# Four reordered places, and the last tiles less their mean on ScalarE beside GpSimd's power

## What is computed

```python
x = x + layernorm(attn0(layernorm(x)))   # attention over the 8 heads of a group, token by token
x = x + layernorm(ffn0(layernorm(x)))    # ternary weights, sigmoid gate
x = x + layernorm(attn1(layernorm(x)))   # 16 heads of 32, causal, rotary embedding
x = x + layernorm(ffn1(layernorm(x)))    # silu gate, 2 of each 4 hidden values kept

def layernorm(x):
    return (x - mean(x)) / sqrt(var(x) + 1e-5)

def ffn1(x):                             # I = 2048
    h = silu(x @ w_gate) * (x @ w_up)
    return keep_two_largest_of_four(h) @ w_down
```

## Time and profile before

| | us |
|---|---|
| median of 3 runs | 1380.36 |
| lowest, highest | 1379.38, 1383.88 |
| the profiled execution | 1379.57 |
| its span in the profile | 1377.8 |
| TensorE busy | 1321.3 (96%) |
| VectorE busy | 981.6 (71%) |
| GpSimd busy | 697.2 (51%) |
| ScalarE busy | 659.4 (48%) |

### The profile page before, as it was taken

How to read it: one execution, slowest core, us unless ns; L and a number is a source line. 1 busy time by engine, 2 the same in 40 slices (tenths; PEclk the granted TensorE clock), 3 DMA queues, 4 the chain that set the end, 5 groups by cost and what they waited for, 6 DMA issues and landing times.

```text
span 1377.8 us, 19437 instructions
## 1 busy us (share of the span) xinstructions
PE 1321.3 (96%) x7181; PEld 911.1 (66%) x7206; DVE 981.6 (71%) x1961; ACT 659.4 (48%) x1149; POOL 697.2 (51%) x836
## 2 busy tenths in 40 slices
PE   6989999999999899999999999999999999999998
PEld 5876446556455455555555457888888788878886
DVE  5898675665767867777666543896779677867787
ACT  6665332232324554455554565645454545455442
POOL 2576231412312424233334276785788668857874
PEclk9999999999999999999999999999999999999999
DMA  9100210103213213034012323122324232322310
GB/s 333 80 1 1 77 62 16 62 31 110 66 46 101 62 41 78 21 108 120 24 55 55 124 93 147 68 94 90 133 83 152 98 134 94 143 104 100 118 36 31
DMA packets 46270, 116.86 MB, mean 85 GB/s; under 512 B 3420, under 2 KB 4448, under 8 KB 42336
## 3 DMA queue, kind: packets, MB, share of 16 engines
q1 hardware_dynamic: 45104, 114.31, 24.5%
q10 hardware_dynamic: 1072, 1.31, 0.3%
HBM read 92.28 MB, written 23.07 MB: 84 GB/s over the span
## 4 chain that ended last, share of the span: by engine, by line
PE 78%; DVE 14%; ACT 4%; issue 2%; POOL 1%; DMA 0%; SPq 0%; POOLq 0%; DVEq 0%; ACTq 0%
PE PS L1796 76%; DVE PS L919 2%; DVE SM L702 2%; PE PS L1805 1%; DVE cm L686 1%; DVE hm L695 1%; DVE SM L698 1%; ACT EX L1369 1%; DVE qb L692 1%; DVE SM L703 1%; DVE tm L686 0%; DVE qa L692 0%; DVE xT L695 0%; DVE SM L692 0%; DVE hm L686 0%
## 5 line engine op out<-in xcount | busy, mean ns | idle before, releaser
L1369 ACT ACTIVATE EX<-PS 128x512 f32<-128x512 f32 (+3 forms) x384 | 169.8, 492 | 134.2 <-PE PS L1796 132.6
L1600 POOL TENSOR_TENSOR ws_g<-rw,ws_g 128x512 fp32r<-128x512 f32 x64 | 134.5, 2102 | 117.5 <-ACT ws_g L1186 117.5
L1600 POOL TENSOR_TENSOR SM<-SM 128x1 f32<-128x1 f32 x128 | 85.4, 667 | 200.5 <-DVE SM L692 197.8
L919 DVE CUSTOM_DVE_ANT_0 PS<-PS,MW 128x128 f32<-128x128 f32 (+3 forms) x256 | 122.3, 503 | 61.6 <-PE PS L1796 61.2
L1796 PE MATMUL PS<-KG,QG 96*128 96x512 f32 (+3 forms) x384 | 134.3, 380 | 17.3 <-DVE SM L919 7.4
L1715 POOL TENSOR_SCALAR_AFFINE_SELECT EX<-EX 128x128 f32<-128x128 f32 x256 | 74.7, 302 | 146.2 <-ACT EX L1369 143.8
L1507 ACT ACTIVATE ab<-hm 128x512 f32<-128x512 f32 x64 | 40.5, 633 | 208.8 <-DVE hm L686 208.8
L1796 PE MATMUL PS<-QG,KG 98*128 98x512 f32 (+3 forms) x384 | 130.3, 374 | 2.1 <-ACT EX L1369 1.7
L686 DVE TENSOR_TENSOR cm<-cm 128x512 bf16<-128x512 bf16 (+1 forms) x136 | 128.3, 973 | 2.4
L1796 PE MATMUL PS<-ws_d,HH 128*128 128x512 f32 x528 | 125.4, 389 | 0.0
L1796 PEld LDWEIGHTS PS<-QG,KG 98*128 98x128 f32 x384 | 69.1, 189 | 69.5 <-issue 43.8
(11 more groups left out here) (204 smaller groups left out, 2782.0 us busy)
## 6 DMA issues: line engine op xcount, KB each, us to landing
rw<-in_L_ffn_w_gate SPq DMA_DIRECT2D x16, 1024.0 KB, 5.0
rw<-in_L_ffn_w_up SPq DMA_DIRECT2D x16, 1024.0 KB, 6.4
rw<-in_L_ffn_w_down SPq DMA_DIRECT2D x16, 1024.0 KB, 7.2
QG<-qs SPq DMA_DIRECT2D x48, 256.0 KB, 4.3
raw<-in_L_ffn_w SPq DMA_DIRECT2D x3, 2816.0 KB, 11.7
qs<-stg SPq DMA_DIRECT2D x16, 512.0 KB, 3.5
xA<-xs SPq DMA_DIRECT2D x2, 2048.0 KB, 7.5
ys<-xA SPq DMA_DIRECT2D x4, 1024.0 KB, 4.2
```

What stands on the lines that cost most here:

```text
L919: last = e.tensor_tensor_reduce(out=p, in0=p, in1=MW[:, 512 - k1 + k0:512], scale=1.0, scalar=BIG, op0=ALU.add, op1=ALU.max, accum_out=m1)
L1369: e.activation(EX[:, n % 16, 0:W], PS[:, score_bank(n), 0:W], ACT.Exp, scale=ISQ, bias=0.0).then_inc(S["ex"], 1)
L1600: return e.tensor_tensor(out, a, b, op)
```

## The change

Five edits:

1. VectorE, last feed-forward: phase 2 of `sparse` is cut in two. The casts stay phase 2 and now stand ahead of the two `turn4`; the subtractions become phase 3 and stay behind them. This differs only at s = 14, 30 and 46.
2. GpSimd, last projection: `stats` of tile step - 2 ahead of `residual` of tile step - 3.
3. ScalarE, second attention: `drain(14)` at n = 358 instead of 360. VectorE's drain 14 stays at 360.
4. ScalarE, second attention: the event `("t3", i)` at its four n stands ahead of `exp(n)` instead of behind it.
5. The last four tiles: VectorE also writes -mean (semaphore `mneg`); GpSimd takes only the power; ScalarE writes the tile less its mean, waiting for `mneg` and not for GpSimd; VectorE then multiplies by the power and adds `xb` in one operation, waiting for both.

```diff
@@ dve_program
+            rounded = [0] * 4
...
-                        n = did(e.tensor_copy(sparse4(q, 0), h[:, r, :]))
+                        rounded[r] = did(e.tensor_copy(sparse4(q, 0), h[:, r, :]))
+                if phase == 3:
                     for r in range(4):
                         q = 4 * g + r
-                        w.wait_ge(S["dvs"], n - 3 + r)
+                        w.wait_ge(S["dvs"], rounded[r])
                         tt(sparse4(q, 1), h[:, r, :], sparse4(q, 0), ALU.subtract).then_inc(S["hh4"], 1)
...
+                if g >= 1 and s % 4 == 2:
+                    sparse(g - 1, 2)
 
                 if k < 3 and s % 16 in (14, 15):
                     i = 4 * (k + 1) + 2 * (s % 16 - 14)
                     turn4(i)
                     turn4(i + 1)
                 if g >= 1 and s % 4 == 2:
-                    sparse(g - 1, 2)
+                    sparse(g - 1, 3)
...
                 stats(124 + i, PS[:, i, :], EPS, "mv8")
+                ts1(col(124 + i, 5), col(124 + i, 0), -1.0, ALU.mult).then_inc(S["mneg"], 1)
...
                 w.wait_ge(S["sn5"], 13 + i)
-                tt(xb[1][:, i, :], xb[1][:, i, :], row4("p", 12 + i), ALU.add).then_inc(S["xo"], 1)
+                w.wait_ge(S["rs8"], 13 + i)
+                stt(xb[1][:, i, :], row4("p", 12 + i), col(124 + i, 4), xb[1][:, i, :], ALU.mult, ALU.add).then_inc(
+                    S["xo"], 1)
@@ act_program
+                    if n in turn_at:
+                        event(("t3", 12 + turn_at.index(n)))
                     exp(n)
                     for t in behind[n]:
-                        event(t)
+                        if t[0] != "t3":
+                            event(t)
...
-                    if n in drain_at:
+                    if n in drain_at and drain_at[n] < 14:
                         drain(drain_at[n])
+                    if n == done_at[14] + 6:
+                        drain(14)
...
-                w.wait_ge(S["rs8"], 13 + i)
+                w.wait_ge(S["mneg"], i + 1)
                 wait_row4("p", 12 + i)
-                norm(row4("p", 12 + i), PS[:, i, :], 124 + i).then_inc(S["sn5"], 1)
+                e.activation(row4("p", 12 + i), PS[:, i, :], ACT.Identity, scale=1.0, bias=col(124 + i, 5)).then_inc(
+                    S["sn5"], 1)
@@ pool_program
-                for k, i in stages(8, 4, step):
-                    if k == 3:
-                        residual(1, i)
-                    if k == 2:
-                        stats(88 + i, "mv6", "rs6", 8 + i)
+                if 2 <= step < 10:
+                    stats(86 + step, "mv6", "rs6", 6 + step)
+                if 3 <= step < 11:
+                    residual(1, step - 3)
...
-                stats(124 + i, "mv8", "rs8", 12 + i)
+                w.wait_ge(S["mv8"], 13 + i)
+                tt(col(124 + i, 4), col(124 + i, 2), mhalf[:, 0:1], ALU.pow).then_inc(S["rs8"], 1)
```

More of the change, by code:

```diff
@@ L45 @@
 pj ue rb rp qh ql d_w0 d_w1 d_k0 d_k1 d_k2 d_k3 d_q00 d_q01 d_q10 d_q11 vj vt vtp va
-sx mxr nm mtp mtl d_m0 d_m1 st ex sel pvd oe de rd oo d_xc cwh cwl
+sx mxr nm mtp mtl d_m0 d_m1 st ex sel pvd oe de rd oo mneg d_xc cwh cwl
 ehi ot ep pc mv6 rs6 en ey d_ys0 d_ys1
```

## The result

| | before | after |
|---|---|---|
| median of 4 runs, us | 1380.12 | 1374.02 |
| lowest, highest, us | 1379.38, 1383.88 | 1373.81, 1374.28 |
| the profiled execution, us | 1379.57 | 1374.02 |
| its span, us | 1377.8 | 1372.3 |

The ratio of after to before is 0.995, with a 95% interval of 0.9937 to 0.9964. The change makes the kernel faster by 0.36 to 0.63%. In part that is luck: terms were wrong in both directions, as the marks on the way show, and one mark that the prediction itself named as a sign of being wrong was missed (edit 3). The table gives when the same instruction starts in the two traces, and what the change gained in the stretch that ends there.

A forecast was written before the change was run, and what follows sets the result against it. TensorE was taken to bound the kernel, so only its waits and the chain behind its last matmul could pay. Terms -2.8 - 1.1 - 0.25 + 0.05 - 1.05 = -5.15 us gave 1374.4, with the median allowance 1374.8; range 1373.3 to 1377.0.

The forecast's parts named there:

- -2.8: Last feed-forward, s = 14, 30, 46: earlier casts end TensorE's three stalls for `hm`, -2.8 us, bounds 2.2 and 2.8.
- (a): At s = 14, 30, 46 another wait takes over, above all ScalarE's queue: 1376.2 (half lost) or 1377.6 us; chance 0.13.
- (e): Last feed-forward: without pauses TensorE's clock falls to its lower level; whole gain gone, or 1385 us; chance 0.03.
- -1.1: Last projection: with GpSimd's statistics first, TensorE's wait ahead of tile 7 goes, -1.1 us, bounds 0.9 to 1.13.
- (b): Last projection: GpSimd's later adds fill the gain from moving its statistics, 1375.9 us; chance 0.08.
- -0.25: Second attention's end: GpSimd's back-to-back selects let ScalarE's earlier drain 14 pass on only 0.25 us, between 0 and 0.8.
- (d): Second attention: ScalarE's earlier drain 14 is handed down in full, 1374.25 us; chance 0.05.
- The other mark: Second attention, near 810 to 815 us: TensorE would show new waits for `EX` by GpSimd.
- +0.05: Second attention, four turned tiles: high half before the exponential gains nothing, `XLb` waits stay; +0.05 us, bounds -0.1 to +0.3.
- -1.05: Last tiles: the closing chain ends 1.10 us sooner, 0.05 lost ahead of it; bounds -1.3 to -0.75.
- (c): Last tiles: GpSimd's power gets in ahead of VectorE's operation and delays it, 1375.4 us; chance 0.08.
- the allowance for the median: Whole kernel: half of the 0.79 us by which the profiled run lay below the median, raising 1374.4 to 1374.8.

The follow-up runs named there:

- one addition: The changed kernel with one more small GpSimd operation (128x1) ahead of the causal select of block 370; one run, 1374.65 us.
- the kernel with another order: The changed kernel with VectorE's row operation of tile 2 ahead of the statistics of tile 3; one run, 1374.89 us.
- the first group of experiments: Four kernels, each the kernel before with one of edits 1, 2, 3 and 5; ratios to before 0.9975, 0.9996, 0.9988 and 0.9992.
- the trace of edit 3: The kernel before with only ScalarE's drain 14 moved two steps earlier; 0.9988 of before, 1378.53 us at the upper clock.

## Why the prediction was right or wrong

The prediction was wrong in a step: it held that GpSimd's selects bound the end of the second attention, so that edit 3 would hand down 0.25 us. TensorE wasn't waiting for them, and 0.80 was handed down. By the prediction's own sign, an attention end more than 0.3 us off, it is wrong. The term of edit 2 was mis-sized by 0.4 besides. The other three terms came within 0.2.

**Edit 1 (-2.8; measured -3.0).** Right in mechanism: the up product follows 2.85 behind the gate product, and `hm` clears it by 0.23 after the 0.15 that a start needed, where 0.2 was forecast. The small error lies behind the waits. The three up products come 0.47, 1.11 and 1.12 sooner behind their gate products, 2.70 in all. But the twelve matmuls behind each wait had taken 2.82 to 2.85 until the next product, and take 2.72 now that there is no wait: 0.35 more, for which the prediction had no term. It can be seen in its rows, 2.98 for the twelve behind the wait and 2.88 without one. Rivals (a) and (e) didn't come.

**Edit 2 (-1.1; measured -0.69).** The term was mis-sized. Tile 7 came as forecast, 2.72 behind tile 6, and there was slightly more to gain than thought (1.18). The 1.13 was 1.04 in the start of tile 7, since tile 1 takes 2.81 (the last matmul overlaps its successor by 0.16, not 0.25), and 0.13 in the twelve matmuls behind the wait, 2.85 instead of 2.72. But the prediction followed the moved statistics to tile 7 and asked of the moved add only what waits for it by semaphore. It didn't lay the add's new time beside VectorE's two-input operations of every tile. Yet it had itself reckoned with such a meeting for tile 7 ("up to 1.3 beside a GpSimd add"), where there was cover; at tile 5, where there was none, the difference took 1.55. Rival (b), the gain filled by GpSimd's later adds, came in part: 0.49 of 1.18, by a way that the prediction hadn't spelled out.

**Edit 3 (-0.25; measured -0.84 to the product, -0.80 to the attention's end; -0.5 to -0.8 there over the kernels with it).** The step that failed is "Since they run back to back GpSimd is behind its own queue, and an earlier exponential doesn't hasten them", with the conclusion that this start isn't handed down. That GpSimd would hardly come earlier was right: its row of eleven selects starts 0.53 sooner, 0.21 of which came ahead of the edit. What was wrong is that this sets the end. The row says that GpSimd had no gaps (it has none from 800.90 on), not that TensorE needed the selects as they came. TensorE's waits by releaser of before, from 797 to 818 us, are a single row:

```profile
PE PS L1796 <- ACT OO L1186: 0.7, 1, 0.7
```

TensorE waited for no select behind drain 14, so an earlier start was handed down until GpSimd's room of 0.5 us was used. The 0.32 from the last select's end to its product, which the prediction took for the most that could pass, wasn't all the room either. The last select took 0.73 where the others take 0.30, beside a two-input difference of VectorE's that started 0.20 ahead of it:

```profile
813.58 0.78 DVE L686 TENSOR_TENSOR OT<-OO,OT 128x512 fp32r<-128x512 f32 x1 [10.02 <-ACT OT L1186]
813.78 0.73 POOL L1715 TENSOR_SCALAR_AFFINE_SELECT EX<-EX 128x128 f32<-128x128 f32 x1
```

In after this difference starts behind a select instead, takes 1.56 itself, and the eleven selects take 2.77 and not 3.19:

```profile
812.53 1.56 DVE L686 TENSOR_TENSOR OT<-OO,OT 128x512 fp32r<-128x512 f32 x1 [8.00 <-ACT OT L1195]
```

Rival (d), with 0.05, was the case, at 0.84 where it said 0.8. The other mark that the prediction named, new waits for `EX` by GpSimd, came only in kernels in which GpSimd was late (0.15 with the row operation of tile 2 first, 0.30 with one addition), and not in after.

**Edit 4 (+0.05; measured -0.05).** The waits stayed, as forecast. The sign was wrong, inside the bounds given.

**Edit 5 (-1.05; measured -0.91 behind the last statistics and 0.03 lost ahead of them, -0.88).** The loss is no firmer than that: in the six traces with after's order it is 0.00 to 0.05, and that the low half `HH` causes it was argued, not shown. The power was forecast to end 0.40 behind VectorE's operation; it ended 0.42 behind it (1368.51 to 1368.93). The 0.19 that the chain fell short of its 1.10 lies in small things: the product and sum took 0.74 and 0.75 where the add with the same operands took 0.69, so that VectorE's first one ended 0.04 later, counted from the statistics, and its last one was 0.06 longer; 0.02 at the power's end; and 0.10 from there to the last start, where I had 0.03. The order didn't turn (rival (c)): VectorE came first by 0.11. The Trainium skill (SBUF — State Buffer, Who interferes with whom) has the later one blocked for the whole of the other's instruction. The 0.55 back in the kernel with another order agrees; a power that ends 0.42 behind VectorE, less than the 0.55 that it takes alone, doesn't quite, as a part of it must have gone on beside.

**The sum.** By stretches 3.0 + 0.69 + 0.84 + 0.06 + 0.88 = 5.5, and the spans differ by 5.5. The forecast had 5.15: edit 3 gave 0.6 more, edit 1 0.2 and edit 4 0.1, and edits 2 and 5 together 0.6 less (0.15 more came ahead of all the edits, which no edit explains). That the terms that were too small and those that were too large nearly cancel is luck. The remaining 0.4 of the 0.8 is the allowance for the median, half of what the profiled run of before lay below it. All four runs of after had a mean granted clock of 0.999 or 1.0, while in the first group of experiments no run of before at that clock took more than 1379.95, so that before's 1380.36 was most likely one at a lower clock; the clock of that run isn't on record.

## What to carry to other kernels

Whether an engine bounds another is read from who waits for it, not from a row without gaps: GpSimd was busy without a gap, and TensorE still showed no wait for it. How much room there is, is told by adding small operations until the wait shows. When a long GpSimd operation is moved, lay its new time beside every two-input VectorE operation near it, for what is lost is not in a semaphore but in a 0.7 us operation that takes 1.55. A pause of TensorE cost more than its idle time: with four pauses of before, the twelve matmuls behind each took 0.10 to 0.13 us longer. A gain is safer to claim where each step has 0.2 us of margin than where two engines' starts lie 0.1 apart.

## What the runs showed of the hardware

Behind drain 14 operations of GpSimd and of VectorE lie beside each other, and each of two durations took one of two values. GpSimd's small product behind the power took 0.77 to 0.79 us or 1.32 to 1.38; the second pair of VectorE's casts took 1.58 to 1.75 or 2.97 to 3.10. All four pairings occur in the fourteen traces, three of them on one chip in kernels with the same instructions up to there. Two of them, in after and in the kernel with one addition:

```profile
799.36 0.77 POOL L1623 TENSOR_SCALAR SM<-SM 128x1 f32<-128x1 f32 x1
...
801.52 3.00 DVE L968 CAST ws_g<-rw 128x512 fp32r<-128x512 f32 x2
```

```profile
799.59 1.33 POOL L1623 TENSOR_SCALAR SM<-SM 128x1 f32<-128x1 f32 x1
...
801.78 1.72 DVE L968 CAST ws_g<-rw 128x512 fp32r<-128x512 f32 x2
```

In kernels with edit 3 and without the addition the triple of selects starts at 10.6 with the short product and the long casts, 10.7 with both short or both long, and 10.8 to 10.9 with the long product and the short casts. The product starts 0.10 ahead of the first casts whether it takes 0.77 or 1.33, so the order of the recorded starts doesn't tell the two apart. What does, stays open.

On one core, too, the time went with TensorE's mean granted clock: the kernel before took 1379.41 at 0.999 or 1.0 (median of 15 runs in the first group), 1381.32 at 0.997 (10), and 1383.5 to 1384.0 at 0.994 or so (4). The traces show what lies behind it. Seven of the fourteen have the upper level (2.4 GHz) from 20 us to the last matmul. In the others the granted clock falls once or twice to its lower level (1.2 GHz, 0.50 in the rows) for 3.4 us. In the trace of edit 3 it does so at 96.9 and at 533.8 us; the third row is the kernel before at the second place (stretch, its length, TensorE busy with the number of matmuls, granted clock, share of the DMA engines, GB/s):

```profile
96.90:100.30 3.40, 3.40 (x14) 0.50 0.00 0
...
533.80:537.20 3.40, 3.40 (x18) 0.50 0.78 180
```

```profile
533.80:537.20 3.40, 3.40 (x28) 1.00 0.79 171
```

One such fall cost about 1.5 us: from the product behind drain 8 to the one behind drain 14 it is 321.8 to 321.9 in the four traces without edit 3 that have no fall there, and 323.4 and 323.6 in the two that have one; with edit 3 it is 321.1 without a fall, 322.5 to 322.6 with one and 323.95 with two. TensorE had been idle for 1.36 us shortly before 533.8 in the trace of edit 3. In the kernel before it was just as idle there, and its clock stayed up, so what brings a fall stays open. The falls lie near 97, 534, 582, 613 and 789 us, none between 800 us and the last matmul, so that the stretches of edits 1, 2 and 5 hold none in any trace; that of edit 3 holds one or two in some, but none in before and after. So under 0.3% two medians of some runs tell less than two stretches of two traces.
